# Expert layers on one core: who makes the low parts of the weights, and in which order VectorE works

## What is computed

```python
pi = _sinkhorn(-(xf @ gate_W.T))
_, top_idx = jax.lax.top_k(pi, 2)
g = jnp.einsum('nd,efd->enf', xf, W_gate)
u = jnp.einsum('nd,efd->enf', xf, W_up)
y = jnp.einsum('enf,edf->end', jax.nn.silu(g) * u, W_down)
for k in range(2):
    out = out + y[top_idx[:, k], n_ar] * pi[:, k:k + 1]
```

## Time and profile before

| | |
|---|---|
| median of 3 executions | 2270.15 us (2267.01 to 2277.14) |
| profiled execution | 2268.48 us |
| its span in the trace | 2266.9 us |
| granted TensorE clock, mean | 0.922 |
| PE busy | 1930.9 us (85%) |
| DVE busy | 1335.8 us (59%) |
| ACT busy | 1381.1 us (61%) |
| POOL busy | 806.4 us (36%) |

### The profile page before, as it was taken

How to read it: one execution, slowest core, us unless ns; L and a number is a source line. 1 busy time by engine, 2 the same in 40 slices (tenths; PEclk the granted TensorE clock), 3 DMA queues, 4 the chain that set the end, 5 groups by cost and what they waited for, 6 DMA issues and landing times.

```text
span 2266.9 us, 37849 instructions
## 1 busy us (share of the span) xinstructions
PE 1930.9 (85%) x11671; PEld 1096.2 (48%) x11671; DVE 1335.8 (59%) x2199; ACT 1381.1 (61%) x1586; POOL 806.4 (36%) x712
## 2 busy tenths in 40 slices
PE   6899999999665497977878778695989999999998
PEld 5722333333424486866766667574742222222245
DVE  4501145456577355444444454443869999999977
ACT  5699999999433122322223222222779999999944
POOL 2011011011201323234132332311128888888932
PEclk9999999999755798988989889897989999999999
DMA  6644344433104544443434434445983535243121
GB/s 204 214 92 66 57 84 84 84 85 85 39 0 170 186 149 158 141 149 122 169 117 171 149 117 172 140 140 191 333 211 57 133 57 133 47 115 70 29 84 67
DMA packets 131069, 276.06 MB, mean 122 GB/s; under 512 B 18588, under 2 KB 69022, under 8 KB 129656
## 3 DMA queue, kind: packets, MB, share of 16 engines
q1 hardware_dynamic: 117160, 228.72, 36.8%
q0 software_dynamic: 6960, 21.77, 3.0%
q10 hardware_dynamic: 6736, 22.94, 2.7%
HBM read 365.58 MB, written 96.21 MB: 204 GB/s over the span
## 4 chain that ended last, share of the span: by engine, by line
PE 29%; ACT 19%; issue 19%; POOLq 16%; DVE 9%; POOL 5%; DMA 3%; ACTq 1%; SPq 0%; DVEq 0%
PE psum L1345 12%; POOLq L2434 10%; PE psum L1326 9%; ACT A1f_probs L1370 8%; ACT A1f_probs L1378 8%; POOLq L2350 5%; POOL e_x L2404 3%; PE psum L381 2%; PE psum L2615 2%; PE psum L850 1%; DMA qk_parts<-L_part 1%; DVE e_hT L2555 1%; PE psum L396 1%; DMA hidden<-e_squares 1%; ACT f_xn L2890 1%
## 5 line engine op out<-in xcount | busy, mean ns | idle before, releaser
L1326 PE MATMUL psum<-A_qa,A_ka 50*128 50x512 f32 x2048 | 408.5, 467 | 22.9 <-DVE A_qa L1413 6.1
L1326 PEld LDWEIGHTS psum<-A_qa,A_ka 50*128 50x128 f32 x2048 | 176.5, 185 | 470.7 <-DVE A1f_probs L1423 243.3
L2615 PE MATMUL psum<-e_w_high,e_hT 128*128 x1136 | 253.0, 315 | 167.5 <-DVE e_hT L2555 160.5
L2615 PE MATMUL psum<-e_w_high,e_xT 128*128 x1136 | 386.3, 403 | 1.9 <-DVE e_xT L2545 1.7
L1547 POOL TENSOR_TENSOR A1f_probs<-A1f_probs,A1f_bias 128x512 f32<-128x512 f32 x256 | 327.5, 1291 | 83.1 <-ACT A1f_probs L1378 82.7
L1423 DVE SCALAR_TENSOR_TENSOR A1f_probs<-psum,A1f_bias 128x1024 f32<-128x1024 f32 x256 | 311.7, 1218 | 23.7 <-PE psum L1326 20.4
L2489 ACT ACTIVATE e_y<-psum 128x256 f32<-128x256 f32 x71 | 27.3, 385 | 482.0 <-PE psum L2615 244.2
L1378 ACT ACTIVATE A0f_probs<-psum 128x1024 f32<-128x1024 f32 x256 | 314.1, 1227 | 0.0
L1366 ACT ACTIVATE A0f_probs<-psum 128x1024 f32<-128x1024 f32 x256 | 312.2, 1219 | 2.5 <-PE psum L1326 2.4
L2615 PEld LDWEIGHTS psum<-e_w_high,e_hT 128*128 128x128 f32 x1136 | 209.3, 220 | 187.1 <-issue 185.9
L1345 PE MATMUL psum<-A1f_probs,v 128*32 128x512 f32 x2048 | 273.9, 606 | 17.5 <-POOL A1f_probs L1547 16.0
(11 more groups left out here) (297 smaller groups left out, 2637.3 us busy)
## 6 DMA issues: line engine op xcount, KB each, us to landing
e_w_raw<-in_experts ACTq DMA_DIRECT2D x67, 3072.0 KB
hidden<-e_squares SPq DMA_DIRECT2D x69, 512.0 KB, 2.9
e_turned<-hidden SPq DMA_DIRECT2D x276, 128.0 KB, 2.7
qk_parts<-L_part SPq DMA_DIRECT2D x64, 512.0 KB, 4.2
A_qa<-qk_parts SPq DMA_DIRECT2D x192, 128.0 KB, 4.3
A_ka<-qk_parts SPq DMA_DIRECT2D x192, 128.0 KB, 6.4
om<-results SPq DMA_DIRECT2D x16, 512.0 KB, 7.7
e_w_raw<-in_experts SPq DMA_DIRECT2D x2, 3072.0 KB, 11.6
```

The source lines that it names most:

```text
L1326: mm = e.matmul(ps[:, side * HALF:(side + 1) * HALF], self.qk.ka[rows, s, pair, kt * P:(kt + 1) * P].bitcast(FP32R), self.qk.qa[rows, s, p ...
L2615: mm = e.matmul(out, left[part].bitcast(FP32R), moving.bitcast(FP32R), start=start and i == 0, stop=stop and i == 2)
```

## The change

The low parts of the weights are made by DVE instead of POOL, the gate and up matrices of a new expert apart: gate at the end of the first new tile, up in the next tile, down in the one after. The DVE order in tile j becomes: `rest_of_hidden(j-2)`, low part of down of j-2, low part of up of j-1, `split_rows(j+1)`, `multiply(j)`, `square(j)`, low part of gate of j. POOL keeps its indirect loads and stores and has no drain any more. `high_part` and the new `low_part` read the buffer's number only inside the branch of a new expert. PE reads `IS_NEW` of each tile beside the buffer's number, and waits for a counter in each tile. The second expert's weights are made at tile 1, 2 or 3 if one of these is the first new tile, and else at the end of tile 3 (`REST` = 4); ACT, DVE and POOL each read the flags for that.

The core of the diff:

```diff
     def pool(self, e):
-        def low_of(buf, a, b): ...
-        def low_second(j): ...
-        def low_part(j, a, b, value):
-            e.wait_ge(self.high_ready, value)
-            buf = bass.ds(self.planned(e, OTHER_BUFFER, j), 1)
-            is_new = self.planned(e, IS_NEW, j)
-            with e.If(is_new > 0):
-                low_of(buf, a, b)
-            e.drain().then_inc(self.low_ready, 1)
+        def fetch_fourth(k):
+            with self.if_second(e, k):
+                e.wait_ge(self.low_ready, self.low_value("second", k))
                 self.fetch(e, 0, FOURTH, 0, self.fourth_in)
...
             if j >= self.LAG:
                 self.store_y(e, j - self.LAG)
-            if j >= 1:
-                low_part(j, 0, DOWN_AT, self.up_ready(j))
-            if j >= self.LAG:
-                low_part(j - 1, DOWN_AT, WIDE, self.down_ready(j - 1))
+            if j + 1 == self.REST:
+                fetch_fourth(self.REST)
...
         def high_part(j, a, b):
-            buf = bass.ds(self.planned(e, OTHER_BUFFER, j), 1)
-            is_new = self.planned(e, IS_NEW, j)
-            with e.If(is_new > 0):
+            with e.If(self.planned(e, IS_NEW, j) > 0):
...
-                high_of(buf, a, b)
+                high_of(bass.ds(self.planned(e, OTHER_BUFFER, j), 1), a, b)
             e.drain().then_inc(self.high_ready, 1)
...
     def dve(self, e, beside):
+        def low_part(j, kind, a, b):
+            with e.If(self.planned(e, IS_NEW, j) > 0):
+                e.wait_ge(self.high_ready, self.high_value("down" if kind == "down" else "up", j))
+                low_of(bass.ds(self.planned(e, OTHER_BUFFER, j), 1), a, b)
+            e.drain().then_inc(self.low_ready, 1)
...
         for j in range(MOE_TILES):
+            if 1 <= j < self.REST:
+                low_second(j)
+            if j >= self.LAG:
+                rest_of_hidden(j - self.LAG)
+            if j > self.LAG:
+                low_part(j - self.LAG, "down", DOWN_AT, WIDE)
+            if j > 1:
+                low_part(j - 1, "up", DC * F, DOWN_AT)
             if j + 1 < MOE_TILES:
                 split_rows(j + 1)
-            if j >= self.LAG:
-                rest_of_hidden(j - self.LAG)
             multiply(j)
             if j < self.BY_PE:
                 square(j)
+            if j:
+                low_part(j, "gate", 0, DC * F)
+            if j + 1 == self.REST:
+                low_second(self.REST)
...
         def wait_for_weights(j):
-            with e.If(buffer_of(j) != buffer_of(j - 1)):
-                e.wait_ge(self.low_ready, self.second_ready(min(j, 2)) if j < 4 else self.up_ready(j - 2))
-                if j > 1:
-                    with e.If(buffer_of(j - 1) != buffer_of(j - 2)):
-                        e.wait_ge(self.low_ready, self.up_ready(j - 1))
+            if j > self.REST:
+                e.wait_ge(self.low_ready, self.low_value("up", j - 2))
+            else:
+                with e.If(is_new(j) > 0):
+                    e.wait_ge(self.low_ready, self.low_value("second", j))
+            if j > 1:
+                with e.If(is_new(j) + is_new(j - 1) > 1):
+                    e.wait_ge(self.low_ready, self.low_value("up", j - 1))
```

More of the change, by code:

```diff
@@ L2316 @@
     BY_PE = MOE_TILES - LAG
+    REST = 4
     Q, R = 4, 32
@@ L2350, in planned, with high_value, low_value, if_second @@
         return e.value_load(self.plan[0:1, row, j:j + 1], min_val=0, max_val=most)
[L2352 to L2360, removed]
+    def high_value(self, kind, j):
+        order = []
+        for k in range(1, MOE_TILES):
+            order += [("second", k)] * (k < self.REST) + [("up", k)] + [("down", k - 1)] * (k > 1)
+            order += [("second", k + 1)] * (k + 1 == self.REST)
+        return order.index((kind, j)) + 1
+    def low_value(self, kind, j):
+        order = []
+        for k in range(1, MOE_TILES):
+            order += [("second", k)] * (k < self.REST) + [("down", k - self.LAG)] * (k > self.LAG)
+            order += [("up", k - 1)] * (k > 1) + [("gate", k)]
+            order += [("second", k + 1)] * (k + 1 == self.REST)
+        order += [("up", MOE_TILES - 1), ("down", MOE_TILES - 2)]
+        return order.index((kind, j)) + 1
+    def if_second(self, e, k):
+        before = [self.planned(e, IS_NEW, i) for i in range(1, min(k + 1, self.REST))]
+        total = before[0]
+        for i, is_new in enumerate(before[1:], 2):
+            if i < k or k == self.REST:
+                total = total + is_new
+        if k == 1:
+            return e.If(before[0] > 0)
+        return e.If(total < 1) if k == self.REST else e.If(before[-1] > total)
     def fetch(self, e, buf, row, j, sem):
@@ L2459, in high_of, with high_second @@
             e.activation(self.w.high[:, buf, a:b].bitcast(FP32R), self.w.raw[:, buf, a:b], ACT.Copy)
[L2461 to L2463 removed]
+        def high_second(k):
+            with self.if_second(e, k):
                 e.wait_ge(self.second_in, DMA)
@@ L2569, in multiply, with low_of, low_second @@
             e.tensor_tensor(out, *parts, ALU.mult).then_inc(self.hidden, 1)
+        def low_of(buf, a, b):
+            e.tensor_tensor(self.w.low[:, buf, a:b].bitcast(FP32R), self.w.raw[:, buf, a:b], self.w.high[:, buf, a:b],
+                            ALU.subtract)
+        def low_second(k):
+            with self.if_second(e, k):
+                e.wait_ge(self.high_ready, self.high_value("second", k))
+                low_of(slice(0, 1), 0, WIDE)
+            e.drain().then_inc(self.low_ready, 1)
[3 more added lines that the diff above has]
+                low_of(bass.ds(self.planned(e, OTHER_BUFFER, j), 1), a, b)
+            e.drain().then_inc(self.low_ready, 1)
         def square(j):
@@ L2654, in down @@
             if j:
-                e.wait_ge(self.low_ready, self.second_ready(1) if j == 1 else self.down_ready(j - 1))
+                e.wait_ge(self.low_ready, self.low_value("second", 1) if j == 1 else self.low_value("down", j - 1))
             if j:
```

28 lines of the change are left out of this document (13 added, 15 removed).

## The result

| | before | after |
|---|---|---|
| median | 2273.25 us (2267.01 to 2277.14, 4 runs) | 2164.22 us (2160.04 to 2167.78, 4 runs) |
| span of the profiled execution | 2266.9 us | 2163.1 us |
| granted clock, mean | 0.922 | 0.937 |

The account below looks back on a forecast made before the run. PE was taken as the bound, with holes mostly at the seven changes of expert. Gains 111 + 12 - 2 + 4.5 + 0.5 = 126 off 2268.5 give 2142.5, plus 1.7 for the median: 2144 us, range 2108 to 2182.

Parts of the forecast that it names:

- three causes: At expert changes: POOL's subtraction stalls DVE's, POOL's drain delays ACT's fetch, long waits lower PE's clock; 23.0 us lost each.
- Part 1: Seven expert changes: without POOL's subtractions and drains each loses 7.2 us instead of 23.0, a gain of 111 us.
- Part 2: Other tiles: cutting the loop through POOL's store and drain to ACT's fetch gains 12 us, between 5 and 16.6.
- Part 5: Start: POOL's 13.13 us job goes and down(2) starts at 785.0 instead of 789.50; gain 4.5 us, between 0 and 7.
- Part 3: DVE's order in quiet tiles: rest_of_hidden ahead of split_rows, with the added reads hidden; price 0.
- slower rival: DVE's register reads make it the bound in every tile, turning at 1.9 us per part; 2394 us at 2.5; chance 0.03.
- Part 4: PE's second register read per tile, 0.75 us, is covered by h_low rising earlier; cost 2 us near the changes.
- The rival in which the second read shows in every tile: PE's added register read isn't hidden in any tile, 38 us less gain: 2182 us; chance 0.10.
- Part 6: Tail after the last tiles: one read less before e_hT, twice; gain 0.5 us.
- DVE takes POOL's place: At expert changes DVE's low parts keep PE's waits at 11 us or more; gain 91, 2179 us; chance 0.14.
- The rival in which nearly everything goes: DVE's jobs fall into idle time and the clock holds, 2.5 us left for a change: 2106 us; chance 0.14.
- The one in which the conflict goes on with POOL's indirect DMAs: POOL's indirect DMAs hold up DVE's larger jobs through the port; gains within 0.5%, about 2265 us; chance 0.02.

Follow-up runs that it names:

- experiment 3: The kernel before, with POOL making only 64 columns of each low part at the seven changes, drains kept: 2178.82 us, ratio 0.9589.
- experiment 4: The kernel before, with POOL draining only behind a low part that it really makes and otherwise raising the counter at once: 2200.69 us, ratio 0.9697.
- experiment 1: The changed kernel, with ACT's refill of raw weights at a change of expert bringing 384 of 6144 columns: 2127.19 us, ratio 0.9364.
- Experiment 6: The changed kernel, with PE reading IS_NEW of each tile once more, a third register read per tile: 2174.04 us, ratio 0.9586.
- experiment 2: The changed kernel, with DVE making only 64 of the 2048 columns of each low part: 2142.38 us, ratio 0.9429.
- experiment 9: The changed kernel, with up's low part behind split_rows, one PE branch on IS_NEW for both counter waits, and PE's registers read earlier: 2165.17 us, ratio 0.9535.

## Why the prediction was right, and which term was mis-sized

**The mechanism of the three causes.** Right. POOL's subtractions at the changes are worth 88 us (experiment 3), the drains that guarded nothing 69 (experiment 4), both as rows of before had them. The trace agrees with what the Trainium skill ("SBUF — State Buffer", "Who interferes with whom") says of VectorE with two SBUF inputs and a GpSimd instruction that reads SBUF: one holds the shared port pair for its whole instruction and the other stands. DVE's subtraction didn't end with POOL's, as the prediction has it, but 1.09 us behind it, both times (1053.65 and 1054.74; 759.29 and 760.38): it did its own work after POOL's.

**The signs.** POOL's busy time, DVE's 2558 (1.28 us at most), the quiet steps and the third step came as the prediction said. The first step was to be 10 to 13 and is 12.5 to 14.5; the fourth was to be 8.6 or 9 and is 12.6 to 15.6. And one of the signs by which the prediction called itself wrong came true: the hidden values' DMAs come late behind the 3 MB fetch.

**Part 1** gave 91 us, not 111: the seven changes lost 165.8 us before (the prediction took 161, seven times the third one) and lose 75.0 now. This is the step that was mis-sized, and it is one term of it:

- *The first step* was to lose 1.3 for `e_hT`, 2.5 for the rows, 0.9 in the next tile and 2.0 for the clock, 6.7 in all. It lost 5.3: 0.76, 2.56 and 2.0, and the 0.9 didn't show. Nearly right, and it would have given 10 us more than forecast.
- *"The 3 MB fetch slows the DMAs of the hidden values, but these are due only two tiles on: 0.5."* **This term is the wrong one**: 5.4 us for a change, 37.8 for seven; experiment 1 takes it all away. The chain from the store to the down product has slack in a quiet tile, but less than the store is late: 8.78 - 2.60 = 6.2 us late, of which 2.45 come out as PE's wait, so the slack is about 3.7 (2.0 to 3.7 over the seven changes). The prediction looked at how long there was until the values were due, and not at how close behind the refill their store would be issued. Before's trace had the warning: with 8.0 us between them store to load took 5.7 instead of 2.6. In the list of what would make the forecast wrong it stood ("if the hidden DMAs come late behind the 3 MB fetch"), but not in the sum.

The term is 34 us too small over seven changes. The first step (10 us) and the 161 (5 us) were off the other way, so Part 1 missed by 20. That the miss stayed so small is luck in part.

**Part 2** gave 11.8, forecast 12. The other tiles lost 11.8 before, not 16.6, and all of it is gone but the one step that belongs to Part 5. Right, and experiment 4 shows the cause: there 0.9 of it is left.

**Part 3** held: the quiet steps are 8.59 to 8.62. DVE's register load takes 305 ns in the middle, and 1204 at its worst, and the quiet steps leave no room for the slower rival (x > 1.9 us for a part).

**Part 4** cost nothing instead of 2. Experiment 6 says how close it was: a third read costs 0.5 us per tile. The rival in which the second read shows in every tile is out for the change; the next read would have shown.

**Part 5** gave 4.5 before the 64 steps, as forecast (turning 793.07 for 797.56), and lost 2.0 of it again within them: 2.5. Its steps: down(0) starts at 755.19 (forecast 753.7), down(2) at 785.53 (forecast 785.0, before 789.50):

```profile
755.19 0.58 PE L2654 MATMUL psum<-e_w_high,e_hT 128*128 x1 [14.63 <-DVE e_hT L2558]
...
785.53 0.58 PE L2654 MATMUL psum<-e_w_high,e_hT 128*128 x1 [9.60 <-DVE e_hT L2558]
```

The 2.0 are the step of 10.59: POOL's late fetch of 3 MB is issued at 785.37, the store of 790.23 behind it goes 8.77 us before its loads, and PE waits for them. It is the top of what was allowed for it.

**Part 6** gave nothing instead of 0.5; what follows the last turning took 1.2 us more. So 91 + 11.8 + 2.5 - 1.2 = 104, the difference of the spans, where 126 was forecast; the medians lie 109 apart.

**The rival "DVE takes POOL's place"** forecast a gain of 91, and the measured 109 lies midway between that and 126: the time alone doesn't tell the two apart, the steps do. It had the size of the loss nearly right (11 to 12 for a change, measured 10.7) and the cause half: DVE's low parts are 5.3 of it, and the other 5.4 is a DMA that no rival named. The rival in which nearly everything goes left 2.5 for a change; measured 10.7. The one in which the conflict goes on with POOL's indirect DMAs is out: DVE's subtraction has a mean of 1.25 us beside 141 of them. By the times it is POOL that stands now: at each change an indirect DMA that starts 1.3 to 1.4 us into a low part of DVE takes 1.7 to 1.9 us instead of 0.98, and the low part still takes 2.3. Nothing was seen to wait for it, as the prediction had it. The third change:

```profile
1013.70 1.90 POOL L2426 DMA_INDIRECT e_x<-token_rows,tokens  x1 [0.30 <-issue]
```

**Why first and late step share.** In the changed kernel the refill goes out 17.8 to 18.3 us after the turning of the change, and the late step ends 25.9 to 28.8 us after the refill, in all seven. The sum less four quiet steps (18.0 + 27.1 - 34.4) is the 10.7 that a change loses. That sum is the four steps by another cut, so the last two columns here must agree but for what the other tiles lose. What is found and not put in is the middle column: it stays at 27 whatever PE does in between, as long as the refill is full:

| | refill after the turning | end of the late step after the refill | 7 x (sum - 34.4) | loss measured |
|---|---|---|---|---|
| changed kernel | 18.0 | 27.1 | 75 | 77.0 |
| 2, small low parts | 14.4 | 27.3 | 51 | 53.2 |
| 9, up behind the rows | 17.9 | 27.2 | 75 | 77.0 |
| 1, small refill | 18.0 | 21.9 (not late) | 38 | 40.8 |

By this, experiment 2 gained by issuing the refill 3.6 us sooner (7 x 3.6 = 25, measured 24), not by its short first steps as such; experiment 9 moved the first steps and left the refill where it was. In 6 PE's own steps use up the same time: late steps of 10 to 11.7. In the other runs with a full refill the middle column is 25.8 to 27.1 on average, with one exception: experiment 4 has 22.0, as experiment 1 has. This reading came after the runs and no run was made for it alone.

**What stays open.** Why the store is held for 8 us or more by 2 MB as by 3, and why its place relative to the refill matters so much, isn't shown. A refill issued behind the loads of the hidden values wasn't tried. One issued some 6 us earlier wasn't tried in the changed kernel, but experiment 4 has it in the kernel before: at six of its changes the refill goes out 8.0 to 8.3 us ahead of the store and the fourth step is 8.6; at the first it goes out 1.3 ahead and the step is 9.9. That speaks for it, no more, since the third step is a long one there. Nor were experiments 3 and 4 put into one run. No version that keeps the weights right beats the changed kernel by more than the measurement tells.

## What to carry to other kernels

When work moves to another engine, follow the counters that it raises: the transfer that they release moves too, and what it meets then is a term of the sum, to be sized from the nearest pair in the trace (here 8.0 us ahead: 5.7; 2.4 us ahead: 8.8), not from how far off the data are due. When a fix shortens one stall and the total doesn't move, look for a later wait that ends at a fixed distance from something else, and measure that distance in both versions. And a drain behind an indirect DMA is not free, even where nothing was computed; sort drains by what stands ahead of them, since one median over all hides the kinds. Before two gains are added or called the same, split the loss by step and see which step each experiment takes.

## What the runs showed of the hardware

- A DVE subtraction with both inputs in SBUF stood while a POOL subtraction ran and ended 1.09 us behind it (9.24 us beside 8.80, 8.04 beside 13.13, else 1.22).
- A POOL drain right behind an indirect DMA took 0.72 to 7.95 us, 2.14 in the middle of 63; seven that started 3.6 us after a 3 MB refill was issued took 4.7 to 5.8. A second drain in the same tile took 0.05. Leaving out those that guarded nothing gained 69 us.
- An indirect DMA of POOL that started inside a 2.3 us subtraction of DVE took 1.7 to 1.9 us instead of 0.98, once in each of seven changes; one that started together with it took 0.98.
- A 512 KB store issued 2.1 to 2.4 us behind a 3 MB load on another engine's queue took 8.5 to 10.5 us until its dependent loads went out, instead of 2.6; issued 8.0 us behind, 4.9 to 6.6. Runs of 1 KB instead of 4 made no difference to the time, and 2 MB delayed it nearly as 3 MB did (8.4 for 9.1 on average).
- On PE two planned register reads for a tile were hidden in tiles of 8.6 us of matmuls; a third showed with 0.5 us or more in every tile (9.06 to 9.3).
- PE's waits of 0.76 and 2.56 us, 5.7 us apart, were followed by a granted clock of 0.50 and left 2.0 us unexplained by the waits themselves; one of 2.45 us was followed by 0.52 and left 1.7.
